# Deformable sampling in a long fused kernel: tile loops written out, and a fifth of the hat functions finished on VectorE

## The reference

```python
def deform_conv2d(x, offset, weight, bias):       # x: 2 x 180 x 96 x 96, ten groups of 18 channels, nine taps
    sy = off[:, :, :, 0] + kys + hh               # per group, tap and pixel
    sx = off[:, :, :, 1] + kxs + ww
    val = (gather(y0, x0, (1 - dy) * (1 - dx)) + gather(y0, x0 + 1, (1 - dy) * dx)
           + gather(y0 + 1, x0, dy * (1 - dx)) + gather(y0 + 1, x0 + 1, dy * dx))
    out = jnp.einsum('bikhw,oik->bohw', patches, weight.reshape(Cout, Cin, KK))
```

## Time and profile before

| | |
|---|---|
| median of three runs | 15135.19 us (15129.42 to 15139.76) |
| the profiled execution, its own time | 15123.16 us |
| its span | 15121.4 us |
| busy over the span | PE 88%, ACT 79%, DVE 77%, POOL 51% |
| the sampling phase, about | 611 us to 9290 us of the span |
| busy in 3000 to 5000 us | PE 1939.1, ACT 1809.1, DVE 1548.7, POOL 1059.1 us |
| granted TensorE clock, whole span | 0.923 |

### The profile page before, as it was taken

One profiled execution on the slowest core, in us unless ns is written; L12 is line 12 of the kernel. 1 busy time (PEld: TensorE's weight loads), 2 busy tenths in 40 slices (PEclk: granted clock), 3 DMA queues, 4 the chain that ended last, 5 costly groups with the idle time before them and its releaser, 6 DMA issues. The chain is left out here.

```text
span 15121.4 us, 248755 instructions
## 1 busy us (share of the span) xinstructions
PE 13339.2 (88%) x80556; PEld 10529.8 (70%) x80556; DVE 11657.3 (77%) x14157; ACT 11922.9 (79%) x17147; POOL 7732.4 (51%) x3946
## 2 busy tenths in 40 slices
PE   7899999999999999999999997565286769999999
PEld 3699999999999999999999995222022225555555
DVE  4577777777777777777777776579776878888888
ACT  2589898898989989898989885129554658999898
POOL 0255555555555555555555553043212447888887
PEclk9999999999999999999999997577687779999999
DMA  4466666666666666666666666524332333333332
GB/s 106 128 164 166 164 168 162 163 167 160 168 162 167 167 162 165 162 167 162 166 161 168 162 162 144 117 85 161 113 96 75 106 105 108 101 107 101 103 101 88
DMA packets 825691, 2102.06 MB, mean 139 GB/s; under 512 B 82811, under 2 KB 439473, under 8 KB 681009
## 3 DMA queue, kind: packets, MB, share of 16 engines
q1 hardware_dynamic: 814289, 2070.18, 52.2%
q10 hardware_dynamic: 9984, 14.16, 0.3%
HBM read 1815.36 MB, written 268.74 MB: 138 GB/s over the span
## 5 line engine op out<-in xcount | busy, mean ns | idle before, releaser
L524 PE MATMUL dc_p<-dc_t 96*128 96x144 f32 x51912 | 6987.2, 289 | 30.5 <-PEq L521 29.0
L584 POOL TENSOR_TENSOR dc_t<-dc_t 128x648 f32<-128x648 f32 x2884 | 4604.7, 1597 | 4687.3 <-POOLq L583 4687.3
L524 PEld LDWEIGHTS dc_p<-dc_t 96*128 96x128 f32 x51912 | 6612.2, 191 | 83.0 <-issue 58.2
L625 DVE TENSOR_TENSOR dc_t<-dc_p,dc_t 128x1296 f32<-128x1296 f32 x2884 | 4344.1, 1506 | 1347.6 <-DVEq L623 1333.3
L463 ACT ACTIVATE dc_t<-dc_t 96x1152 f32<-96x1152 f32 x2886 | 3595.6, 1246 | 115.1 <-ACTq L462 114.8
L465 ACT ACTIVATE dc_t<-dc_t 96x1152 f32<-96x1152 f32 x2886 | 3360.0, 1164 | 354.0
L1977 DVE TENSOR_TENSOR_SCAN ms_t<-ms_t,ms_p 128x512 f32<-128x512 f32 x1728 | 2129.9, 1271 | 281.7 <-PE ms_p L1919 205.0
L1893 POOL TENSOR_TENSOR ms_t<-ms_t 128x1536 f32<-128x1536 f32 x576 | 1988.0, 3456 | 504.3 <-DVE ms_t L1977 500.5
L640 DVE TENSOR_TENSOR dc_t<-dc_t 128x324 f32<-128x324 f32 x2883 | 1426.3, 495 | 631.1 <-DVEq L638 593.0
L1929 PE MATMUL ms_p<-ms_t,top_t 128*128 128x512 f32 x3456 | 1776.0, 596 | 0.0
L561 PE MATMUL dc_p<-dc_t 128*128 128x180 f32 (+1 forms) x7488 | 1666.0, 322 | 69.5 <-PEq L556 49.9
(11 more groups left out here) (207 smaller groups left out, 10648.5 us busy)
## 6 DMA issues: line engine op xcount, KB each, us to landing
dc_t<-sxd SPq DMA_DIRECT2D x1443, 864.0 KB, 5.7
ms_t<-bcd SPq DMA_DIRECT2D x576, 256.0 KB, 3.3
dc_t<-xrT SPq DMA_DIRECT2D x145, 675.0 KB, 5.6
kvd<-wk_t SPq DMA_DIRECT2D x18, 1536.0 KB, 5.1
xvd<-mi_t SPq DMA_DIRECT2D x36, 768.0 KB, 3.5
szd<-mi_t SPq DMA_DIRECT2D x36, 768.0 KB, 5.7
dld<-mi_t SPq DMA_DIRECT2D x36, 768.0 KB, 3.4
ms_t<-dld SPq DMA_DIRECT2D x36, 768.0 KB, 6.9
```

The source lines that it names most:

```text
L524: ins = e.matmul(PT[j % 2][:, t // 3, (t % 3) * 144:(t % 3 + 1) * 144], HX[:, m % NHX, t * 128:(t + 1) * 128], XW[:, i, ky:ky + WIN, g * C ...
L584: e.tensor_tensor(z[:, :, 0:HALF], z[:, :, 0:HALF], z[:, :, HALF:2 * HALF], ALU.add)\
L625: e.tensor_tensor(Zt[:, n % 4, :].rearrange("p (b m i) -> p b m i", b=3, i=CG), PT[n % 2][:, :, 0:432].rearrange("p b (m i) -> p b m i", i ...
```

## The change

Three things are changed in `sample_and_convolve`.

1. The loop over the 18 bodies of an image becomes a Python loop, so the program holds 36 copies of the body where it held two. The loop over row windows stays a hardware loop. The addresses on SP are worked out from constants accordingly.
2. For groups 2 and 7 (`TURNED`), ACT makes only the distance. DVE makes min(distance, 1) - 1 from it, which is the hat with its sign turned (`turn_hats`, for step n + 3 in turn n, between `quarter` and `sum_rows`, so at n mod 10 = 4 and 9). The sign is put right by turning the row hats of the same groups as well (`turn_rows`, one instruction for each half of a tile's row hats, at n mod 20 = 19 and 2).
3. PE gives one more count of `s_bxf` before its first body, so every broadcast load can start one pair sooner.

```diff
+    TURNED = (2, 7)
...
-                with e.Fori(0, NT // NRB) as y2:
+                for y2 in range(NT // NRB):
                     with e.Fori(0, nw) as w:
                         body(b, y2, w)
...
-                e.wait_ge(s_bxf, 2).then_inc(s_bxf, -2)
+                e.wait_ge(s_bxf, 3).then_inc(s_bxf, -3)
...
-                    e.activation(BX[:, q, u, :], BX[:, q, u, :], ACT.Abs, bias=QX[:, 0:1]).then_inc(s_ab, 1)
-                    e.wait_ge(s_ab, 1).then_inc(s_ab, -1)
-                    e.activation(HX[:, slot, :], BX[:, q, u, :], ACT.Relu, bias=1.0, scale=-1.0)\
-                        .then_inc(s_hx, 1)
+                    if j % NG in TURNED:
+                        e.activation(BX[:, q, u, :], BX[:, q, u, :], ACT.Abs, bias=QX[:, 0:1]).then_inc(s_dist, 1)
+                    else:
+                        e.activation(BX[:, q, u, :], BX[:, q, u, :], ACT.Abs, bias=QX[:, 0:1]).then_inc(s_ab, 1)
+                        e.wait_ge(s_ab, 1).then_inc(s_ab, -1)
+                        e.activation(HX[:, slot, :], BX[:, q, u, :], ACT.Relu, bias=1.0, scale=-1.0)\
+                            .then_inc(s_hx, 1)
...
-                    e.wait_ge(s_hx, 1).then_inc(s_hx, -1)
+                    if g in TURNED:
+                        e.wait_ge(s_hd, 1).then_inc(s_hd, -1)
+                    else:
+                        e.wait_ge(s_hx, 1).then_inc(s_hx, -1)
...
                     sample(j)
+                e.sem_inc(s_bxf, 1)
...
                     if j % NG == 0:
-                        e.wait_ge(s_hy, 1).then_inc(s_hy, -1)
+                        e.wait_ge(s_ng, 1).then_inc(s_ng, -1)
...
+                def turn_hats(j):
+
+                    e.wait_ge(s_dist, 1).then_inc(s_dist, -1)
+                    e.tensor_scalar(HX[:, j % NBB % NHX, :], BX[:, j // 2 % 5, j % 2, :], 1.0, 1.0, ALU.min, ALU.subtract)\
+                        .then_inc(s_hd, 1)
+
+                def turn_rows(i, h):
+
+                    e.wait_ge(s_hy, 1).then_inc(s_hy, -1)
+                    hy = HY[:, i, h * HM:(h + 1) * HM, :].rearrange("p (g t) r -> p g (t r)", g=NG)[:, 2:NG:5, :]
+                    e.tensor_scalar(hy, hy, -1.0, None, ALU.mult).then_inc(s_ng, 1)
...
                             add_up((n - 13) // NB, (n - 13) // NG % 2)
+                        if n % NB == 19:
+                            turn_rows((n // NB + 1) % 2, 0)
+                        if n % NB == 2:
+                            turn_rows(n // NB % 2, 1)
+                        if (n + 3) % NG in TURNED:
+                            turn_hats(n + 3)
                         sum_rows(n - 2)
```

More of the change, by code:

```diff
@@ L376, in sample_and_convolve @@
         PF = p.ps([128, 512])
-        s_w, s_hy, s_ab, s_hx, s_t, s_z, s_va, s_tr, s_vt, s_bxf, s_f, s_ff, s_out, s_fin, s_rw, s_hyf, s_pt, s_va2, s_half, s_qt, s_sum = p.sems(21)
+        s_w, s_hy, s_ab, s_hx, s_t, s_z, s_va, s_tr, s_vt, s_bxf, s_f, s_ff, s_out, s_fin, s_rw, s_hyf, s_pt, s_va2, s_half, s_qt, s_sum, s_dist, s_hd, s_ng = p.sems(24)
         s_xw = p.sems(2)
@@ L426, in body @@
                     for i in range(NRB):
-                        y = e.snap(y2 * NRB + i)
-                        first = e.snap((y + ((y * 43) >> 7)) * near + w * WIN + s0)
-                        ti = e.snap(y * NWIN + w + t0)
+                        y = y2 * NRB + i
+                        first = e.snap(near * (y + ((y * 43) >> 7)) + w * WIN + s0)
+                        ti = e.snap(t0 + w + y * NWIN)
                         row_loads(i, b, ti, y)
@@ L436, in body @@
                             if q == 6:
-                                done = y if i else e.snap(y2 * NRB + ((w + 15) >> 4) * NRB)
+                                done = b * NT + y if i else e.snap(((w + 15) >> 4) * NRB + (b * NT + y))
                                 last = (i - 1) % NRB
-                                store_tile(last, e.snap(done + b * NT), s_st[last % 2])
+                                store_tile(last, done, s_st[last % 2])
                 loops(e, body)
@@ L662, in _ @@
                     rows(0, h)
+                for h in range(2):
+                    turn_rows(0, h)
+                turn_hats(2)
                 weigh(0)
```

## The result

The changed kernel takes 15294.09 us (median, 15286.13 to 15301.76), against 15132.31 us for the one before: ratio 1.0107, 95% interval 1.0089 to 1.0124. It is slower by 162 us, where 214 were forecast. The profiled execution has a span of 15297.6 us.

The account below looks back on a forecast made before the run. Bound: the closed loop through POOL and DVE. A tile: 57.26 + 2.84 + 1.35 + 0.30 = 61.75 us; 144 tiles 8892 us against 8677.6, +214 us, so 15349 us; range for 8 in 10, 15150 to 15580.

Parts of the forecast that it names:

- The bound: Closed loop of POOL's `halve` and DVE's `quarter` and `sum_rows`: 2.80 us a plain turn, 56.0 us a tile.
- The restarts: Hardware loop over bodies: 34 restarts of 9.15 us each, clock's share included; written out, all go, saving 311 us.
- The sign named for it: Restarts gone would show as no idle time over 1 us in front of L550's weight loads.
- Relu leaves ACT: Four of 20 Relus a tile leave ACT, removing all 0.84 us of lateness over the 57.26 us floor.
- The floor of 57.26: Tile without lateness: 56.0 us for 20 turns, 0.62 for two `add_up`, 0.64 for two first `rows`.
- `turn_hats`: Four DVE operations a tile in the closed loop: 0.80 us each, 0.71 after overlap, 2.84 us a tile.
- The rival at the pace of PSUM: `turn_hats` on DVE takes 1.38 us, 334 us more in all, total 15683 us; chance 6%.
- Its wait for the distance: DVE's `turn_hats` waits for ACT's distance: 0.37, 0.1, 0.37, 0.5 us in turns 14, 9, 4, 19; sum 1.35.
- What was put at nothing: PE's wait for turned hats (made two turns before need), SP's earlier loads and SP's registers: no cost.
- The work is not hidden: Rival: the loop through POOL has slack hiding the new DVE work, only restarts count, 14824 us; chance 10%.
- the waits don't vanish: Rival: waits of `turn_hats` vanish, its operation a bit cheaper, additions about 3.1 us a tile, 15160 us; chance 6%.
- the loop change does something: Rival: writing out the tile loops does nothing, as the inner loop also breaks the instruction stream; 15660 us, chance 5%.

Follow-up runs that it names:

- the fastest kernel: The changed kernel with DVE's order weigh, turn_rows or turn_hats(n + 2), sum_rows, quarter, add_up: 14513.30 us, ratio 0.9599 to the kernel before.

## Why the prediction held

**The bound.** The closed loop from `halve` over `quarter` and `sum_rows` back to `halve`, 2.80 us, holds a turn in the changed kernel as in the old one. Four experiments speak for it: the same DVE work moved out of it saves 248 us beyond its waits; a wait removed from it saves its full length; when the step from DVE back to POOL shrinks from 0.36 to 0.30 us, the turn shrinks with it; and `quarter` taken out of it, with no turned hats, shortens a tile from 57.54 to 56.56 us. The last also shows how little the loop was ahead of PE: about 1 us a tile.

**The restarts**, 311 us: 307 measured alone, 295 on top of the change. The sign named for it, no idle time over 1 us in front of PE's transposes, was badly chosen: the restarts are gone, but the turned turns leave gaps of up to 1.7 us.

**Relu leaves ACT**, all of the 0.84 us of lateness gone. The sum was nearly right and the reason wrong. The lateness over 57.26 us was 0.76 us with the loops alone, and 0.48 of it went with the earlier loads, with every Relu still on ACT. Turned hats had at most 0.28 left to gain, and there is no sign that they gained it: by my means over all tiles a plain turn is 2.81 us with them and without. The floor of 57.26, added up from single turns, was itself too low by about as much: plain turns are 2.81 on average and not 2.80, those with `add_up` or `rows` 3.12 to 3.14.

**`turn_hats`**, 0.80 us and 0.71 in the loop: 0.756 and 0.67 to 0.68. The estimate of 0.69 us from the Trainium skill (VectorE: DVE Perf Modes, perf-mode tier table) was 0.07 too low, mine of 0.80 was 0.04 too high. The rival at the pace of PSUM falls.

**Its wait for the distance** is the term that was mis-sized: 1.35 us a tile predicted, 0.94 measured by removing it, or 0.24 for each turned hat, where the prediction named an average far from 0.34 as a sign of being wrong. Turns 14 and 4 had 0.37 and 0.27 for 0.37 each; turn 9 none for 0.1; turn 19 0.29 for 0.5 (my averages over all tiles, from the distance between `quarter` and `turn_hats` less 0.41, and less 0.15 for `turn_rows`). That is 144 x 0.41 = 59 us too much.

**`turn_rows`**, 0.15 each: 0.228 us long, 0.14 to 0.15 in the loop.

**What was put at nothing.** PE waited 0.5 us in the whole phase for hats. They were made one turn before PE needs them and not two, as the prediction says, and even made in the same turn, a turn later, they cost it nothing.

**How near the sum came** is in part luck. A measured tile is 57.54 without turned hats, 2.92 for the new work and 0.94 for the waits, 61.40 us; the prediction had 57.26, 3.14 and 1.35, 61.75 us. The base was 0.28 too low, the work 0.22 and the waits 0.41 too high. The first two nearly cancel, so that the miss of 50 us in the phase (15349 against 15294 in the whole) is about the size of the waits' alone.

**The rivals.** The work is not hidden, the waits don't vanish, and the loop change does something; all three fell, as did the pace of PSUM. The granted clock stayed at 1.00, 2.4 GHz, with PE's new gaps of up to 1.7 us.

## What to carry to other kernels

An idle time that is the same in every turn points to a closed loop between engines. Walk it once: every instruction put between its links costs nearly its whole duration (here all but 0.09 us), however idle the engine is. Before work is moved to a less busy engine, find a place outside that loop; the same six instructions a tile cost 547 us inside it, 426 of them without their waits, and gained 89 once the loop was open. And before a wait that looks needless is taken out, look at what it keeps apart.

## What the runs showed of the hardware that I had not expected

A DVE addition with two inputs in SBUF that starts 0.15 us after a POOL addition lasts until 0.18 us past its end, 1.68 in place of 0.32 us; the same order on one-input operations stretches 0.228 to 1.59 us, and 0.756 to 2.12. When DVE's 0.76 us start 0.33 us ahead, POOL is only 0.29 us longer; when `rows`, 0.90 us, starts 0.02 us ahead, as in the fastest kernel, `halve` takes 2.31 us (medians). The order of two starts, a fraction of a microsecond apart, decides between 14593 and 16555 us for the whole kernel.
